# Four-block sequence model on one core: other work beside the first two and the last two scans

## The chip, the cores and the metric

The kernel runs on one core of one Trainium2 chip. The metric is device time in microseconds (us) of one execution. Its engines are TensorE (PE in the profile; PEld is its weight load), VectorE (DVE), ScalarE (ACT), GpSimd (POOL) and SyncE (SP), which here only issues DMAs.

## The reference, cut to what matters

Four blocks follow each other on x of 32 sequences, 256 positions, 256 channels, in float32. Each takes its scale, shift and gate from a condition vector. Blocks 1 and 3 are selective state-space layers (block 1 on permuted positions), 2 is softmax attention with 16 heads, 4 linear attention.

```python
def mamba(h):                                   # blocks 1 and 3
    xm, z = split(h @ W_in)                     # 512 channels each
    xm = silu(causal_conv4(xm) + conv_b)
    dtr, Bm, Cm = split(xm @ W_xp)              # 64, 16, 16
    dt = softplus(dtr @ W_dt + b_dt)
    def step(hst, t):                           # over 256 positions
        hst = hst * exp(dt[t] * A) + (dt[t] * xm[t]) * Bm[t]
        return hst, sum_over_16(hst * Cm[t])
    y = (scan(step) + xm * D) * silu(z)
    return y @ W_out
x = x + gate * unpermute(mamba(permute(mod(layernorm(x)))))    # block 1
x = x + silu(mod(layernorm(softmax(q @ k.T + mask) @ v))) @ W  # block 2
x = x + gate * mamba(mod(layernorm(x)))                        # block 3
x = x + silu(mod(layernorm(q_soft @ (k_soft.T @ v)))) @ W      # block 4
```

## The kernel before

The 32 sequences go in 16 groups of two (`NG = 16`), so a group's row of positions has 512 elements. Everything of a group stays in the core; each group passes through pieces of work:

- `front0` / `front1`: normalisation, input projection, convolution and silu of block 1 / block 3, in `front_tensor`, `front_scalar`, `front_vector` (lines 660 to 900).
- `mid0` / `mid1`: the projection w_xp (L722), its copy `xd` (L834), the rows B and C written to memory by SP (L1124), and the first of four step sizes `dt` (L886) and their products `dtx` (L909).
- `rest0` / `rest1`: the other three step sizes and the gate branch `sz` (L855).
- `scan0` / `scan1`: the recurrence of block 1 / block 3 in 32 steps. One step is, on DVE, a product with a slice of B (L1025) and a hardware scan (L1039), on ACT two exponentials (L975), on POOL the product with C (L1057) and an add (L1064), on PE an accumulation through the identity (L926). The slices of B and C come by DMA from memory, spread over the partitions (L1097). After each eight steps DVE gates a chunk of 128 channels (L1008).
- `back0` / `back1`: output projection (L1139), for block 1 the permutation back (L1149), gate (L1177) and residual sum (L1185).
- `attn_a` / `attn_b`: block 2 of the group's first / second sequence. A chain: statistics (L623), transposes (L1207), q, k, v (L1231, L1222), sixteen maxima of scores (L1277 on PE, L1397 on DVE), scores again transposed (L1304), exponentials (L1372), product with v (L1320), reciprocal (L1409), normalisation, output, and the sum into x_b (L1421).
- `lin_a` / `lin_b`: block 4 of the group's first / second sequence, with the result stored.

`scan0` and `scan1` alternate. A recurrence of one group is accompanied by other pieces of neighbouring groups. These stand in two lanes, `SIDE`; pieces of a lane follow each other and share its buffers. An entry is (piece, offset of its group from the iteration i, 0 or 1 for beside scan0(i) or scan1(i - 1)). In an iteration a piece whose group doesn't exist is left out, and so is a scan:

```python
SIDE = [[("attn_b", -1, 0), ("front1", -1, 0), ("back0", 0, 1), ("attn_a", 0, 1), ("front0", 1, 1)],
        [("rest0", 0, 0), ("back1", -2, 0), ("lin_a", -2, 0), ("mid1", -1, 0),
         ("rest1", -1, 1), ("lin_b", -2, 1), ("mid0", 1, 1)]]
SCAN = [("scan0", 0), ("scan1", -1)]
```

The order on each engine is fixed when the program is made. `PLACES[piece][engine]` has a number for each part of a piece, in units of scan steps: 8.4 stands between the operations of step 8. `iteration` merges the scan's own places (`AT`) with those of both lanes, smallest first. Every engine then works through its list strictly in order, waiting on semaphores for its inputs and for buffers. PLACES decides what may run beside what, and a part that waits holds up all behind it on its engine, the scan's steps included.

So before, back0(0), attn_a(0), front0(1) and mid0(1) stand in an iteration half in which scan1(-1) doesn't exist, and attn_b(15), front1(15), back1(14), lin_a(14) and mid1(15) in one in which scan0(16) doesn't exist. Where a scan has no successor beside it, its last two accumulations, its last POOL operations and its last gated product come at once.

`keep_result` (line 606) is a DMA that ACT issues, the copy of x_b, the attention's result, to `x_scratch` in memory; `back1` loads it again later. `scan_sync` issues the slices of B and C, `front_sync` the taps of the convolution and `mid_sync` the B and C rows, all on SP.

## Time and profile before

| | us |
|---|---|
| median of three runs | 5471.16 |
| the three runs | 5450.6, 5471.16, 5473.3 |
| the profiled execution | 5456.22 |
| its span, first to last instruction | 5454.5 |
| busy in it: PE, DVE, POOL, ACT | 4531.0, 4640.3, 4057.9, 3256.7 |

The span begins with a prologue and front0(0), mid0(0), up to the first step of scan0(0) at 122.3 us. Then 32 scans follow one another, the last of which ends at 5344.4. In the rows below the times count from the span's start, "granted clock" (PEclk) is the share of TensorE's full clock of 2.4 GHz that it had, a mean over the stretch where it changed in it (0.5 is the lower level of 1.2 GHz), and a figure in brackets with an arrow is the idle time of the engine ahead of an instruction and what ended it.

### The profile page before, as it was taken

The page shows a single profiled execution, that of the slowest core. Times are in us where ns is not written, and L with a number is a line of the kernel's source. Part 1 is how long each engine was busy: PE and PEld are TensorE (multiplying, and loading weights), DVE is VectorE, ACT ScalarE, POOL GpSimd, SP SyncE. Part 2 cuts the span into 40 slices and gives each one's busy share as a digit, 9 for nine tenths or more (in the row PEclk, how much of TensorE's full clock was granted, in tenths as well). Part 3 has the DMA queues.
Part 4 walks back from the last instruction along what each step waited for, and adds up shares of the span by engine and source line. Part 5 has one row for each costly group of instructions (what it writes and reads, how often), then busy time and mean ns, then how long its engine had stood idle before and what let it go on. Part 6 is the DMA issues. An engine that isn't in the chain of part 4 may idle for free.

```text
span 5454.5 us, 54997 instructions
## 1 busy us (share of the span) xinstructions
PE 4531.0 (83%) x16792; PEld 2409.9 (44%) x16792; DVE 4640.3 (85%) x4711; ACT 3256.7 (60%) x5572; POOL 4057.9 (74%) x2838
## 2 busy tenths in 40 slices
PE   4678888888888898888888888888889888888765
PEld 1243444444444444444444444444444444444423
DVE  2729899998999999999999999899999999999373
ACT  2336566666666666666666666666666666666252
POOL 1818787887878888787788788787878878787172
PEclk8668899999999999998999999999999999998776
DMA  4616666676766666676666667676666667666161
GB/s 144 221 44 233 224 237 223 232 240 215 240 214 240 229 232 229 226 252 220 229 224 236 230 232 239 217 244 214 239 229 234 229 225 250 218 229 219 45 206 58
DMA packets 355068, 1164.54 MB, mean 214 GB/s; under 512 B 39355, under 2 KB 79348, under 8 KB 354774
## 3 DMA queue, kind: packets, MB, share of 16 engines
q1 hardware_dynamic: 310614, 1106.42, 59.9%
q10 hardware_dynamic: 44160, 54.60, 3.1%
q8 instruction: 135, 2.21, 0.2%
q14 instruction: 159, 1.30, 0.1%
HBM read 1140.78 MB, written 20.10 MB: 213 GB/s over the span
## 4 chain that ended last, share of the span: by engine, by line
PE 43%; DVE 19%; POOL 11%; issue 10%; ACT 9%; DMA 5%; SPq 1%; DVEq 0%; POOLq 0%; ACTq 0%
DVE hw L1039 8%; PE ps L926 7%; PE ps L698 6%; POOL hw L1057 6%; PE ps L1231 5%; PE ps L1277 5%; PE ps L1304 4%; DVE ps L1025 3%; PE ps L1222 3%; POOL hw L1064 3%; DMA cs<-bc_scratch 2%; PE ps L1139 2%; PE ps L1320 2%; ACT da L975 2%; DVE mx L1397 2%
## 5 line engine op out<-in xcount | busy, mean ns | idle before, releaser
L1057 POOL TENSOR_TENSOR hw<-hw,cs 128x1024 f32<-128x1024 f32 x1024 | 2413.1, 2357 | 668.9 <-DVE hw L1039 604.2
L1039 DVE TENSOR_TENSOR_SCAN hw<-da,ps 128x1024 f32<-128x1024 f32 x1024 | 2333.4, 2279 | 66.1 <-ACT da L975 23.5
L975 ACT ACTIVATE da<-dt,a_neg 128x510 f32<-128x510 f32 x2048 | 1332.0, 711 | 175.2 <-DVE hw L1039 171.9
L1064 POOL TENSOR_TENSOR hw<-hw 128x512 f32<-128x512 f32 x1024 | 1298.1, 1268 | 66.3
L926 PE MATMUL ps<-hw,ident 128*128 128x512 f32 x2048 | 1177.7, 680 | 172.7 <-POOL hw L1064 172.7
L1025 DVE TENSOR_TENSOR ps<-ps,bs 128x1024 f32<-128x1024 f32 x1024 | 1255.9, 1226 | 38.8 <-ACT ps L989 11.3
L926 PEld LDWEIGHTS ps<-hw,ident 128*128 128x128 f32 x2048 | 398.6, 212 | 621.8 <-issue 322.6
L698 PE MATMUL ps<-hT,w_in 128*128 128x512 f32 x1024 | 532.7, 657 | 67.8 <-DVE dt L886 47.8
L1372 ACT ACTIVATE pts<-ps 128x512 f32<-128x512 f32 x512 | 278.5, 593 | 428.5 <-PE ps L1304 428.5
L1397 DVE TENSOR_REDUCE mx<-ps 128x2 f32<-128x512 f32 x512 | 330.9, 680 | 164.2 <-PE ps L1277 163.7
L1277 PE MATMUL ps<-k,q 32*128 32x256 f32 x2048 | 347.1, 464 | 106.1 <-DVE mx L1397 106.1
L570 ACT ACT_TABLE_LOAD x319 | 409.3, 1283 | 5.7
L698 PEld LDWEIGHTS ps<-hT,w_in 128*128 128x128 f32 x1024 | 200.4, 205 | 343.6 <-issue 208.8
L1277 PEld LDWEIGHTS ps<-k,q 32*128 32x128 f32 x2048 | 203.5, 214 | 298.8 <-DVE mx L1397 191.6
L1304 PE MATMUL ps<-q,k 32*128 32x256 f32 x2048 | 301.4, 413 | 15.4 <-ACT pts L1372 15.4
L1320 PE MATMUL ps<-pts,va 128*32 128x256 f32 x2048 | 271.2, 398 | 2.8 <-ACT pts L1372 2.8
L909 POOL TENSOR_TENSOR dtx<-dt,u 128x512 f32<-128x512 f32 x128 | 162.2, 1267 | 139.8 <-DVE dt L886 139.7
L1304 PEld LDWEIGHTS ps<-q,k 32*128 32x128 f32 x2048 | 180.9, 190 | 142.7 <-issue 60.2
L1139 PE MATMUL ps<-w_out,dtx 128*128 128x256 f32 x1024 | 240.2, 389 | 3.4 <-DVE dtx L1008 1.8
L713 PE MATMUL ps<-xd,w_dt 97*128 97x512 f32 x256 | 168.1, 744 | 76.8 <-POOL dtx L909 53.4
L707 PE MATMUL ps<-u,taps 128*128 128x512 f32 (+3 forms) x512 | 229.1, 590 | 0.0
L1139 PEld LDWEIGHTS ps<-w_out,dtx 128*128 128x128 f32 x1024 | 195.8, 194 | 57.6 <-issue 30.7
(178 smaller groups left out, 5296.6 us busy)
## 6 DMA issues: line engine op xcount, KB each, us to landing
bs<-bc_scratch SPq DMA_DIRECT2D x1024, 512.0 KB, 4.3
cs<-bc_scratch SPq DMA_DIRECT2D x1024, 512.0 KB, 4.9
taps<-taps_scratch SPq DMA_DIRECT2D x32, 512.0 KB, 5.6
xhat<-in_x ACTq DMA_DIRECT2D x16, 512.0 KB, 7.7
gate<-gates_scratch ACTq DMA_DIRECT2D x64, 128.0 KB, 5.1
x_b<-in_x ACTq DMA_DIRECT2D x16, 512.0 KB, 6.6
x_scratch<-x_b ACTq DMA_DIRECT2D x16, 512.0 KB, 2.9
x_c<-x_scratch ACTq DMA_DIRECT2D x16, 512.0 KB, 6.5
```

The lines of the kernel that those rows point to most:

```text
L570: nc.scalar.preload_act_table_set(name)
L698: ins = nc.tensor.matmul(side[pc.bank[f"m{m}"]], w_in[l][:, k, m * P:(m + 1) * P], hT[:, k, :], start=(k == 0), stop=(k == DC - 1))
L926: nc.tensor.matmul(yps, ident[:, :], hw[q % RING][:, 0, :], start=False, stop=(q % PER == PER - 1))\
L975: ins = nc.scalar.activation(da[q % (AHEAD + 1)][:, k, :, 1:S], dt_[:, c, :].rearrange("p (b s) -> p b s", b=GB)[:, :, 1:S], ACT.Exp, scal ...
L1025: nc.vector.tensor_tensor(z, dxp.unsqueeze(1).broadcast_to([P, 2, T]), bs[s % B_RING][:, :, :], ALU.mult)\
L1039: nc.vector.tensor_tensor_scan(tile[:, :, :].rearrange("p n t -> p (n t)"), da[s % (AHEAD + 1)][:, :, :, :].rearrange("p n b s -> p (n b s)"),
L1057: nc.gpsimd.tensor_tensor(tile[:, :, :], tile[:, :, :], cs[s % C_RING][:, :, :], ALU.mult)\
L1064: nc.gpsimd.tensor_tensor(tile[:, 0, :], tile[:, 0, :], tile[:, 1, :], ALU.add)\
L1139: ins = nc.tensor.matmul(side[pc.bank[key]][:, k * D:(k + 1) * D], dtx[l][:, c, r * P:(r + 1) * P], w_out[l][:, c, :], start=(c == 0), sto ...
L1277: ins = nc.tensor.matmul(banks[hh][:, t * S:(t + 1) * S], q4[rr, h // 4, t * P:(t + 1) * P], k4[rr, h // 4, :], start=True, stop=True)
L1304: ins = nc.tensor.matmul(banks[hh][:, t * S:(t + 1) * S], k4[rr, h // 4, t * P:(t + 1) * P], q4[rr, h // 4, :], start=True, stop=True)
L1397: nc.vector.tensor_reduce(mx[:, :, h // 4, at0], side[pc.bank[f"s{p}{hh}"]].rearrange("p (t s) -> p t s", t=RB), X, ALU.max, negate=True). ...
```

## The change

`SIDE`, `SCAN` and the iterations go. `PLAN` lists the segments one by one, each with its scan, its two lanes and the name of a table of places:

```diff
+def even(i):
+    return step((0, i), [("attn_b", i - 1), ("front1", i - 1)],
+                [("rest0", i), ("back1", i - 2), ("lin_a", i - 2), ("mid1", i - 1)], "even")
+def odd(i):
+    return step((1, i - 1), [("back0", i), ("attn_a", i), ("front0", i + 1)],
+                [("rest1", i - 1), ("lin_b", i - 2), ("mid0", i + 1)], "odd")
+PLAN = [odd(-1),
+        step((0, 0), [("front0", 1)], [("rest0", 0)], "first"),
+        step((0, 1), [("back0", 0), ("attn_a", 0), ("attn_b", 0), ("front1", 0)],
+             [("mid0", 1), ("rest0", 1), ("mid1", 0)], "second"),
+        odd(1)]
+for _i in range(2, NG - 1):
+    PLAN += [even(_i), odd(_i)]
+PLAN += [even(NG - 1),
+         step((1, NG - 2), [("back0", NG - 1), ("attn_a", NG - 1), ("attn_b", NG - 1), ("front1", NG - 1)],
+              [("rest1", NG - 2), ("lin_b", NG - 3)], "last_but_one"),
+         step((1, NG - 1), [], [("back1", NG - 2), ("mid1", NG - 1), ("rest1", NG - 1), ("lin_a", NG - 2),
+                                ("lin_b", NG - 2)], "last"),
+         step(None, [], [("back1", NG - 1), ("lin_a", NG - 1), ("lin_b", NG - 1)], "end")]
```

The tables "even" and "odd" have the numbers that `PLACES` had. "first", "second", "last_but_one", "last" and "end" are new, with places such as

```diff
+    "second": {
+        "mid0": {
+            "pe": [-100.8, -100.6, -100.4, -100.2, 0.208, 0.833],
+        "front1": {
+            "dve": [29.732, 29.866, 30.041, 30.082, 30.124, 30.165, 30.206, 30.247, 30.289],
```

where a negative place stands ahead of the scan's first step. Two more edits reach every scan:

```diff
@@ front_scalar
             ln_apply(act, lane_a, pc, g, lambda r: x_src[l][:, r, :], R)
-            if l == 1:
-                keep_result(act, g)
@@ mid_scalar, behind the copy xd
+            if l == 1:
+                keep_result(act, g)
@@ scan_vector and scan_sync
-            yield 0
+            yield -2
```

The second sorts the first B slice of a scan (place -0.8) ahead of pieces with a later negative place, on SP. The waits for shared buffers are written with one function, `prior(l, g)`, that names the recurrence before a given one, in place of `near`, `latest` and `before_scan`; they wait for what they waited for. `segment` merges places as `iteration` did, and `flush` has the last operations of a scan without a successor.

The order of instructions shows three places. On PE, from the end of scan0(0) to attention of group 0. Names: `hw` is the scan's tile, `w_xp` and `xd` belong to mid0(1), `w_out` and `xhat,onehot` to back0(0). Before:

```order
L941 MATMUL ps<-u,diag_d 128x512
L926 MATMUL ps<-hw,ident 128x512 x8
L1139 MATMUL ps<-w_out,dtx 128x256 x16
L1149 MATMUL ps<-xhat,onehot 128x256 x8
L1207 MATMUL ps<-ident,xhat 128x128 x4
```

After:

```order
L1121 MATMUL ps<-hw,ident 128x512 x7
L917 MATMUL ps<-u,w_xp 96x512 x4
L908 MATMUL ps<-xd,w_dt 128x512
L1334 MATMUL ps<-w_out,dtx 128x256 x16
L1344 MATMUL ps<-xhat,onehot 128x256 x8
L908 MATMUL ps<-xd,w_dt 128x512
```

mid0(1) has moved ahead of back0(0), and attention now begins behind the second low-rank product, beside scan0(1).

On DVE, attention into front of block 3, near the end of the packed scan0(1) (`mx` the maxima, `q` their sum into q, `rec` the reciprocal, `u` a convolution tap, `ps<-ps,bs` and `hw<-da,ps` a scan step). Before, of attn_a(0) and front0(1), in the stretch without a scan:

```order
L1397 TENSOR_REDUCE mx<-ps 128x2 x16
L1404 TENSOR_TENSOR q<-q,ps 128x512 x2
L1409 RECIPROCAL rec<-ps 128x16
L1411 TENSOR_TENSOR xhat<-ps,rec 128x256
```

After, of attn_b(0), front1(0) and mid1(0), in scan0(1):

```order
L1592 TENSOR_REDUCE mx<-ps 128x2 x13
L1599 TENSOR_TENSOR q<-q,ps 128x512 x2
L1220 TENSOR_TENSOR ps<-ps,bs 128x1024
L1234 SCALAR_TENSOR_TENSOR hw<-da,ps 128x1024
L1220 TENSOR_TENSOR ps<-ps,bs 128x1024
L1604 RECIPROCAL rec<-ps 128x16
...
L1073 SCALAR_TENSOR_TENSOR u<-ps,cols,u 128x2x253
L1234 SCALAR_TENSOR_TENSOR hw<-da,ps 128x1024
L1081 SCALAR_TENSOR_TENSOR dt<-ps,dt 128x512
L1220 TENSOR_TENSOR ps<-ps,bs 128x1024
L1234 SCALAR_TENSOR_TENSOR hw<-da,ps 128x1024
```

The links of the chain now alternate with scan steps; the scan's last three steps stand behind attn_b's reciprocals, front1's taps and mid1's dt.

On SP, where one scan passes into the next in the middle (`bc_scratch<-xd` writes the B and C rows, `bs` and `cs` are slices of them). Before:

```order
L1124 DMA bc_scratch<-xd 32x512
L1097 DMA cs<-bc_scratch 128x1024
L1114 DMA taps<-taps_scratch 128x1024
L1097 DMA bs<-bc_scratch 128x1024 x2
```

After:

```order
L1319 DMA bc_scratch<-xd 32x512
L1292 DMA cs<-bc_scratch 128x1024
L1292 DMA bs<-bc_scratch 128x1024
L1309 DMA taps<-taps_scratch 128x1024
L1292 DMA bs<-bc_scratch 128x1024
```

The load of the taps has moved behind the scan's first B slice.

## Rows read from the trace of the kernel before

**Rows 1.** Busy time by stretches: stretch, length, engines busy (instructions), clock, DMA share, GB/s.
```profile
core 0: us, PE busy (x) PEld busy (x) DVE busy (x) ACT busy (x) POOL busy (x), PEclk, DMA share, GB/s
122.30:244.40 122.10, 73.30 (x90) 21.13 (x88) 115.75 (x70) 56.60 (x84) 112.54 (x64) 0.61 0.81 271
244.40:395.60 151.20, 109.56 (x379) 62.38 (x380) 27.17 (x60) 35.33 (x67) 11.99 (x20) 0.67 0.05 16
395.60:542.50 146.90, 117.84 (x410) 55.91 (x408) 134.41 (x116) 91.45 (x154) 120.73 (x77) 0.86 0.70 239
2261.40:2412.90 151.50, 133.55 (x513) 70.26 (x513) 142.85 (x146) 98.34 (x173) 125.55 (x88) 0.94 0.68 239
2412.90:2573.10 160.20, 139.58 (x533) 76.90 (x533) 145.30 (x146) 105.05 (x178) 127.78 (x90) 0.92 0.66 223
4908.30:5062.10 153.80, 123.84 (x475) 68.35 (x475) 139.21 (x130) 91.24 (x156) 124.68 (x85) 0.84 0.66 223
5062.10:5208.10 146.00, 107.71 (x423) 61.37 (x423) 34.37 (x77) 46.44 (x89) 12.01 (x24) 0.78 0.08 25
5208.10:5344.40 136.30, 83.24 (x155) 34.41 (x155) 120.93 (x91) 68.14 (x106) 116.19 (x72) 0.68 0.73 244
```

**Rows 2.** The page's costliest groups: busy us, mean ns of one, idle before.
```profile
L1057 POOL TENSOR_TENSOR hw<-hw,cs 128x1024 f32<-128x1024 f32 x1024 | 2413.1, 2357 | 668.9 <-DVE hw L1039 604.2
...
L1064 POOL TENSOR_TENSOR hw<-hw 128x512 f32<-128x512 f32 x1024 | 1298.1, 1268 | 66.3
```

**Rows 3.** Timeline of DVE, first stretch without a scan: start, length, instruction.
```profile
264.69 0.70 DVE L1177 TENSOR_TENSOR ps<-ps,gate 128x512 f32<-128x512 f32 x1 [11.62 <-PE ps L1149]
...
267.87 0.75 DVE L623 BATCH_NORM_STATS2 stats<-x_b 128x6 f32<-128x256 f32 x2
...
352.17 0.69 DVE L1421 TENSOR_TENSOR x_b<-ps,x_b 128x512 f32<-128x512 f32 x1 [8.27 <-PE ps L1222]
357.09 1.41 DVE L623 BATCH_NORM_STATS2 stats<-xhat 128x6 f32<-128x256 f32 x4 [4.23 <-DMA xhat<-in_x]
...
381.42 2.31 DVE L878 SCALAR_TENSOR_TENSOR u<-ps,cols,u 128x510 f32<-128x510 f32 x3 [4.54 <-ACT u L779]
392.59 0.69 DVE L886 SCALAR_TENSOR_TENSOR dt<-ps,dt 128x512 f32<-128x512 f32 x1 [8.86 <-ACT dt L823]
...
395.56 1.23 DVE L1025 TENSOR_TENSOR ps<-ps,bs 128x1024 f32<-128x1024 f32 x1 [1.28 <-ACT ps L989]
```

**Rows 4.** Timeline of PE, same stretch: back0(0), then mid0(1).
```profile
253.22 9.61 PE L1139 MATMUL ps<-w_out,dtx 128*128 128x256 f32 x32 [0.88 <-DVE dtx L1008]
...
383.82 3.60 PE L722 MATMUL ps<-u,w_xp 128*96 128x512 f32 x8
388.10 1.12 PE L713 MATMUL ps<-xd,w_dt 97*128 97x512 f32 x2 [0.68 <-ACT xd L834]
```

**Rows 5.** Timeline of DVE, second stretch without a scan.
```profile
5069.14 0.74 DVE L623 BATCH_NORM_STATS2 stats<-x_b 128x6 f32<-128x256 f32 x2
...
5153.14 0.69 DVE L1421 TENSOR_TENSOR x_b<-ps,x_b 128x512 f32<-128x512 f32 x1 [5.61 <-PE ps L1222]
...
5201.05 0.69 DVE L886 SCALAR_TENSOR_TENSOR dt<-ps,dt 128x512 f32<-128x512 f32 x1 [9.03 <-ACT dt L823]
...
5208.12 1.22 DVE L1025 TENSOR_TENSOR ps<-ps,bs 128x1024 f32<-128x1024 f32 x1
```

**Rows 6.** Timeline of DVE: ends of two attention chains beside scans.
```profile
570.14 0.75 DVE L623 BATCH_NORM_STATS2 stats<-x_b 128x6 f32<-128x256 f32 x2
...
650.08 0.69 DVE L1421 TENSOR_TENSOR x_b<-ps,x_b 128x512 f32<-128x512 f32 x1 [2.32 <-PE ps L1222]
...
698.25 0.73 DVE L623 BATCH_NORM_STATS2 stats<-x_b 128x6 f32<-128x256 f32 x2
...
793.28 0.69 DVE L1421 TENSOR_TENSOR x_b<-ps,x_b 128x512 f32<-128x512 f32 x1
```

**Rows 7.** Waits of DVE from 1641.7 to 4442.8: total us, times, longest.
```profile
DVE ps L1025 <- DMA bs<-bc_scratch: 3.3, 9, 1.0
```

More of the change, by code:

```diff
@@ new lines, in step @@
+def step(scan, lane_a, lane_b, table):
+    lanes = [[(name, g) for name, g in lane if 0 <= g < NG] for lane in (lane_a, lane_b)]
+    return scan if scan and 0 <= scan[1] < NG else None, lanes, table
+def even(i):
[4 more added lines that the diff above has]
+                [("rest1", i - 1), ("lin_b", i - 2), ("mid0", i + 1)], "odd")
@@ L516, in build @@
         x_src, x_res = [xhat, x_b], [x_b, x_c]
-        near, table = {}, {}
+        table = {"now": None}
         def number(name, g):
```

533 lines of the change are left out of this document (344 added, 189 removed), and 18 rows, old and new, of the table PLACES.

## The prediction, made before the changed kernel ran

> **What bounds the kernel now.** I read the busy time by stretches first [rows 1]. The scans are the long stretches: in the middle one takes 151.5 to 160.2 us, with DVE busy for 142.9 and 145.3 of it, PE for 134 to 140 and POOL for 126 to 128. No engine is idle there for long, and only a small part of the change touches them. A scan alone has a floor: POOL's two operations for each of the 32 steps take 2.357 + 1.268 = 3.63 us, 116 us in all [rows 2], and scan0 of group 0, with only rest0 beside it, lasts 122.1 us [rows 1].
>
> The other thing in these rows is two stretches without any scan: 244.4 to 395.6 (151.2 us) and 5062.1 to 5208.1 (146.0 us). POOL works for 12.0 us in each, DVE for 27 and 34, DMA stands at 0.05 and 0.08. What runs is one chain, its links waiting for each other. I followed it on DVE, where each link leaves a row. In the first stretch: gate of back0 at 264.69, statistics of attn_a at 267.87, its result x_b finished at 352.17 + 0.69 = 352.9, so **85.0 us of attention chain**; front0 from 357.09 to the last convolution tap at 381.42 + 2.31 = 383.7, **26.6 us**; the step size dt at 392.59; the first step of scan0(1) at 395.56 [rows 3]. In the second: statistics of attn_b at 5069.14, result at 5153.8, 84.7 us; dt at 5201.05, first step of scan1(15) at 5208.12 [rows 5]. The change attacks exactly these, so its value is the length of the two stretches less what the packed scans grow.
>
> **How long a chain takes beside a scan** is the number on which everything rests, and before has it: attn_a of group 1 beside scan1(0) from 570.14 to 650.08 + 0.69 is 80.6 us, attn_b of the same group beside scan0(2) from 698.25 to 794.0 is 95.7 us [rows 6]. Bare it is 85. So a chain loses little to a scan beside it, and the scan goes on meanwhile. But one scan of 116 to 122 us cannot cover two such chains, a front and a mid: 85 + 85 + 27 + 9 is 206 us bare. Each packed scan ends when its chain does, not when POOL does.
>
> **Front of the program, part by part**, from the last step of scan0(0) at 244.4 to the end of the stretch at 542.5, where scan1(0) begins: 298.1 us before [rows 1]. After:
> (a) front0(1) moves beside scan0(0). On DVE it adds statistics 1.41, two small operations of about 0.5, and six taps at 2.31 / 3, 4.6 in all: 6.5 us [rows 3]. DVE was busy for 115.75 of 122.1 us and has no room for it, so +6.5 (2 if the waits hide it, 12 if taps wait for PE). Its work on PE and ACT (73.3 and 56.6 us busy there) is hidden; if that cover were gone, it would be the 26.6 us of the bare front.
> (b) The junction. Before, the last scan ends at 244.4 and the gate starts at 264.69, 20.3 us. Now PE has mid0(1) in front of back0: four projections and a low-rank product, 383.82 to 389.22, 5.4 us [rows 4], of which a little falls into the wait for the last gated product. I take +5. From gate to statistics it was 3.2 us; scan0(1)'s first multiplication (1.2 us) now stands between. Statistics start 30 us after the scan's end.
> (c) attn_a and attn_b one after the other. attn_a is paced by eight scan steps ahead of its first maxima, so I take 90, between 80.6 and 95.7. attn_b has its last twenty-odd DVE operations crowded between four scan steps and runs nearly bare: 88, between 84.7 and 95.7. Together 178 (161 to 191).
> (d) front1(0) has to end before the scan's step 30, since its taps stand ahead of it on DVE: 26.6 us bare, 30 with steps between (26 to 36, which is two and a half steps of 3.63 more).
> (e) mid1(0): last tap to dt 392.59 - 383.73 = 8.9, and dt to the next scan's first step 5208.12 - 5201.05 = 7.1 [rows 3, 5], under which the last scan step of 3.6 us is hidden.
> Sum 6.5 + 30 + 178 + 30 + 16 = 260.5. **Saved 37.6 us.** Nothing is gained twice: the 146.9 us of scan0(1) [rows 1] vanish into this chain.
>
> **End of the program**, from 4908.3 to 5208.1, 299.8 us before [rows 1]. After: three scan steps (11 us) and back0's gate and sums stand ahead of attn_a's statistics, with a wait for PE about 20 us (16 to 28). Then 178 for the two chains. Step 31 is done right after the second chain's result, so front1(15) runs bare but for that step: 30. New in the chain is back1(14), which DVE and PE have ahead of mid1(15): the last gated product 0.7, two groups of 16 products (9.61 us for 32, so 4.8 each) [rows 4], gate and sum 1.5 between them, since the second group waits for the first sum: 12. Then mid1: projections to dt 8.8, dt to the first step 3.0 [rows 3, 4]. Sum 20 + 178 + 30 + 12 + 11.8 = 251.8, **saved 48.0**. Against it, the last scan gets lin_a(14) beside lin_b(14). One lin chain and a different rest are what divides the last scan's 136.3 us from the first one's 122.1, so 14.2, while DVE's busy time differs by 5.2 only [rows 1]. The second lin costs between these: I take 11, nearer the whole. Net 37.0. The last stretch, 5344.4 to the end, holds the same chain in the same order: 0.
>
> **Middle.** On PE, DVE and POOL its instructions keep their order. On SP the first B slice of a scan is issued ahead of the taps; DVE waited for such a slice 9 times for 3.3 us in nine pairs of scans [rows 7], so at most some 5 us over the whole. On ACT the copy of x_b to memory comes after mid1's xd instead of after the front's normalisation. It lands there beside the write and the read of the B and C rows; it isn't waited for until the next back1. Its cover is the 0.66 to 0.68 share of DMA [rows 1]. I take -3 together (-5 to +15).
>
> **The sum.** 37.6 + 37.0 + 3 = 77.6 us. Against the profiled execution's own time, 5456.2 (span 5454.5), that is 5378.6. The three runs gave 5450.6, 5471.2 and 5473.3; the profiled one lies 15 us under their median. What is saved should carry over, so the forecast is 5471.2 - 77.6 = **5394 us** (1.4% less).
>
> **TensorE's clock** could move it. The granted clock is 0.67 and 0.78 in the two stretches without a scan, between the levels of 1.2 and 2.4 GHz, 0.86 in scan0(1) and 0.92 to 0.94 in the full middle scans [rows 1]: the busier PE is, the higher. That would speed the very links that move beside a scan. The Trainium skill, page "TensorE: Matmul & The Clock Gate", section "What's actually happening", says that the low clock is the default and that activity lifts it; these rows agree. By that rule alone all four chains would run as the quickest does, which is the first rival below.
>
> **Rivals.**
> 1. *Chains at the higher clock.* In a packed scan PE has work from the scan, rest, back, attention and front, and grants like the middle's 0.92. Then each chain takes the 80.6 us of [rows 6] rather than 90 and 88: 16.8 less in each of two packed scans, 33.6 together, 5360. For it speaks that table; against it, that 13 maxima in a row and the whole second half of attn_b's products stand on PE and DVE with hardly a scan step between, as bare as in the old stretch.
> 2. *Chains as slow as the slowest.* 95.7 us each, as attn_b beside scan0(2), where DVE's and ACT's order makes each link wait for scan steps: 13.4 more in each packed scan, and fronts of 36 rather than 30, 12 more: 5433. For it speaks that steps and links alternate in a fixed order; against it, that attn_b here has fewer steps among its links than in rows 6.
> 3. *Slower than before: the overlap fails.* Place: both packed scans. All engines work in a fixed order, and where a crowd of links stands ahead of a scan step, POOL runs dry and the steps come after the chain. My sum hides all 116 us of scan in each chain. What isn't hidden adds to the time: with half of it exposed, 2 x 58 = 116, 5510. It decides from one third exposed (78 of 232). Against it: rows 6, where scan and chain do go together, and bare chains of 85 that leave POOL idle.
> 4. *It touches the middle after all.* The copy to x_scratch meets the B rows at the start of 14 scans; at 1.5 us each that is 21 us, 5415. Rows 7 show how little slack a B slice has in every second scan; DMA at two thirds speaks against much.
>
> **How the numbers follow.** Chances: forecast 0.48, rival 1 0.20, rival 2 0.22, rival 3 0.04, rival 4 0.06. The terms of the forecast cannot all err the same way; two thirds of their spread give 5370 to 5420. The range reaches over rival 1's time and to rival 2's with its edges, 5340 to 5440. About 0.5% (27 us) is what a measurement of this kernel can tell from no change: under 5444 lie the forecast, rival 1, and most of 2 and 4: faster 0.88; the far edge of 2 and 4 gives same 0.08; slower 0.04 is rival 3.
>
> **What the changed kernel's profile would show.** Right: scan0(0) at 125 to 134 us; first to last step of scan0(1) some 215 to 235 us with the next scan starting near 505 instead of 542.5; scan1(14) some 190 to 205 us, scan1(15) at 141 to 150 us and beginning about 250 us after scan0(15) ends; attention chains of 80 to 96 us, back to back; middle scans as in rows 1 to a microsecond. Wrong: chains over 100 us (rival 2 or 3), POOL idle in long pieces with steps 25 to 31 stacked behind the chain and still to come after it, a granted clock over 0.9 with chains of 80 (rival 1), or middle scans longer by 1 us or more (rival 4).

## The result, and the profile after

The changed kernel takes 5421.34 us (median of six runs, 5411.25 to 5426.06); the kernel before, timed beside it, takes 5460.54 us (5448.15 to 5473.3). The ratio is 0.9925 with a 95% interval of 0.9908 to 0.9943: 39 us faster, where the forecast said 77.6. The time lies inside the predicted range. The profiled execution has a span of 5424.3 us against 5454.5, 30.2 us less and not 39, since the profiled run of before lies 4.3 us under its median and that of the changed kernel 4.7 above; a second trace of the changed kernel has a span of 5413.5 us. In what follows ratios are over the fast runs alone; one slow run each of e1 (6018.8 us) and e5 (6429.0 us) counts in their medians only.

Busy time of the changed kernel by stretches (columns as in [rows 1]): scan0(0); the junction; scan0(1) with both attention chains of group 0 and front1(0); the middle; scan1(14) with both chains of group 15; the stretch behind it; scan1(15). The last line is the middle of the kernel before.

```profile
core 0: us, PE busy (x) PEld busy (x) DVE busy (x) ACT busy (x) POOL busy (x), PEclk, DMA share, GB/s
126.30:248.70 122.40, 81.65 (x136) 30.51 (x136) 118.98 (x77) 65.85 (x96) 116.20 (x69) 0.74 0.79 266
248.70:270.60 21.90, 18.70 (x56) 11.08 (x57) 2.11 (x4) 5.58 (x9) 4.96 (x4) 0.83 0.33 109
270.60:513.30 242.70, 195.05 (x685) 97.82 (x683) 154.89 (x155) 114.64 (x194) 121.26 (x85) 0.77 0.41 141
515.40:4892.10 4376.70, 3809.93 (x14577) 2048.83 (x14577) 4026.54 (x4039) 2826.66 (x4847) 3541.50 (x2455) 0.93 0.68 230
4896.40:5129.90 233.50, 191.74 (x739) 108.91 (x739) 156.79 (x170) 100.84 (x185) 123.75 (x94) 0.77 0.42 141
5129.90:5175.00 45.10, 32.71 (x89) 17.37 (x90) 8.63 (x13) 13.23 (x23) 5.71 (x4) 0.88 0.18 63
5175.00:5318.70 143.70, 92.06 (x218) 45.95 (x217) 128.40 (x111) 76.94 (x129) 119.88 (x81) 0.74 0.68 229
...
542.50:4908.30 4365.80, 3805.72 (x14577) 2045.65 (x14577) 4026.60 (x4039) 2827.22 (x4846) 3540.83 (x2455) 0.93 0.68 230
```

The overlap is there: DVE and POOL now do a scan's work, 121 and 124 us of POOL, under the chains, and the long stretches in which POOL stood idle are gone. But the packed scans last 242.7 and 233.5 us, and the granted clock in both is 0.77, where a full middle scan has 0.92 to 0.94 [rows 1].

The chain's marks on DVE (start, length, instruction), as in [rows 3] and [rows 5]: statistics and result of attn_a(0) and attn_b(0), then of attn_a(15) and attn_b(15).

```profile
273.90 0.75 DVE L818 BATCH_NORM_STATS2 stats<-x_b 128x6 f32<-128x256 f32 x2
...
385.17 0.69 DVE L1616 TENSOR_TENSOR x_b<-ps,x_b 128x512 f32<-128x512 f32 x1 [1.48 <-PE ps L1417]
386.91 0.74 DVE L818 BATCH_NORM_STATS2 stats<-x_b 128x6 f32<-128x256 f32 x2
...
476.72 0.69 DVE L1616 TENSOR_TENSOR x_b<-ps,x_b 128x512 f32<-128x512 f32 x1 [5.89 <-PE ps L1417]
...
4920.94 0.75 DVE L818 BATCH_NORM_STATS2 stats<-x_b 128x6 f32<-128x256 f32 x2
...
5030.93 0.67 DVE L1616 TENSOR_TENSOR x_b<-ps,x_b 128x512 f32<-128x512 f32 x1
5032.64 0.74 DVE L818 BATCH_NORM_STATS2 stats<-x_b 128x6 f32<-128x256 f32 x2
...
5124.97 0.69 DVE L1616 TENSOR_TENSOR x_b<-ps,x_b 128x512 f32<-128x512 f32 x1 [8.27 <-PE ps L1417]
```

attn_a(0) takes 112.0 us and attn_b(0) 90.5; attn_a(15) takes 110.7 and attn_b(15) 93.0. The forecast had 90 and 88. So the first block's chain is 22.0 and 20.7 us too long in the two packed scans, 42.7 us of the 47.4 by which the traces fall short of the forecast. The table behind the experiments has the other terms.

One term came out near the forecast's size, but for another reason. The chain that leads to the first step of scan0(0) (start, length, what):

```profile
116.92 7.44 DMA xhat<-in_x
...
124.48 1.42 DVE stats L818 x4
...
126.36 1.12 DVE ps L1220
```

front0(1) now has its statistics on DVE ahead of the first scan step, and they wait for its input, which lands at 124.4. scan0(0) begins at 126.3 instead of 122.3.

### The profile page after: what moved, and what is told of

Its sections match the earlier page's. It is cut to its first block, busy times and chain, and to the rows that moved or that the text cites. A ratio compares the mean times of both kernels' runs of the same rounds, so it can differ in the third digit from the quotient of the medians.

```text
span 5424.3 us, 55001 instructions
## 1 busy us (share of the span) xinstructions
PE 4533.2 (84%) x16792; PEld 2421.1 (45%) x16792; DVE 4642.0 (86%) x4711; ACT 3257.2 (60%) x5574; POOL 4057.2 (75%) x2838
## 4 chain that ended last, share of the span: by engine, by line
PE 44%; DVE 20%; POOL 11%; issue 10%; ACT 9%; DMA 5%; SPq 1%; DVEq 0%; ACTq 0%; POOLq 0%
DVE hw L1234 8%; PE ps L1121 8%; PE ps L893 6%; POOL hw L1252 5%; PE ps L1426 5%; PE ps L1472 5%; PE ps L1499 4%; DVE ps L1220 3%; PE ps L1417 3%; POOL hw L1259 3%; PE ps L1515 2%; PE ps L1334 2%; ACT da L1170 2%; DVE mx L1592 2%; DMA cs<-bc_scratch 2%
## 5 line engine op out<-in xcount | busy, mean ns | idle before, releaser
L902 PE MATMUL ps<-u,taps 128*128 128x512 f32 (+3 forms) x512 | 231.1, 594 | 0.0
L1334 PEld LDWEIGHTS ps<-w_out,dtx 128*128 128x128 f32 x1024 | 192.8, 191 | 60.2 <-issue 32.3
```

Of the source, the lines that this page charges most:

```text
L1334: ins = nc.tensor.matmul(side[pc.bank[key]][:, k * D:(k + 1) * D], dtx[l][:, c, r * P:(r + 1) * P], w_out[l][:, c, :], start=(c == 0), sto ...
```

## The experiments

Two theories stood at the start. The first: a chain's links take their turn in a fixed order behind the scan's steps and other pieces, on DVE, ACT and PE alike, and the first block's chain has more of that beside it. The second: PE sets the chain's pace, by its clock and by the scan's sums. Beside them stood the question of the middle, 10.9 us longer. Differences of packed scans under 4 us are not read: a second trace of the same kernel (the last but one run below) moves that much.

**e1, e2: each end alone.** The lines of `PLAN` are those of after at one end and those of before at the other.

```diff
 PLAN += [even(NG - 1),
-         step((1, NG - 2), [("back0", NG - 1), ("attn_a", NG - 1), ("attn_b", NG - 1), ("front1", NG - 1)],
...
+         odd(NG - 1),
+         step(None, [("attn_b", NG - 1), ("front1", NG - 1)], [("back1", NG - 2), ("lin_a", NG - 2), ("mid1", NG - 1)],
```

> Only the front is rearranged; the last two groups' scans and chains keep the order of the kernel before. Theory by stretches (the traces of before and after, added up): the prologue gives back 4.0 us and the stretch between the first two scans saves 31.4, so 27 us in all, 5433 against 5460. Rival A, the moved copies and pieces inside the unchanged middle cost the 10.9 us by which that middle grew: this kernel has them too, so it saves 16 us, about 5444. Rival B, the forecast on record: 37.6 us, 5423. The middle of the trace tells A from the first theory: 4366 or 4377 us from the start of the second layer's first scan to the end of the last scan of the first layer. The attention chain of block 0 beside the scan should again take 108 to 116 us and that of block 1 88 to 93, since nothing in the front differs from after.

> Only the end is rearranged; the front keeps the order of the kernel before. Theory by stretches: the stretch between the last scan of the first layer and the last scan saves 16.9 us, the last scan costs 7.4, what follows it saves 4.5: 14 us, 5446 against 5460. Rival A, the grown middle (10.9 us) belongs to the moved copies: 3 us, 5457. Rival B, the forecast on record: 37 us, 5423. The chain of block 0 of the last group should again take about 110 us and that of block 1 about 93.

Front alone: ratio 0.996 (0.9945 to 0.9976), 5440.7 us against 5459.6; scan1(0) begins at 514.1 us, 28.4 earlier than before. End alone: 0.9989 (0.9968 to 1.001), 5456.6 us; from the end of scan0(15) to the end of the last scan 426.1 us for 436.1, and 105.6 for 110.1 behind it. These marks repeat those of after to 2 us, and by them the front has two thirds of the saving. The medians add up to 22 us of after's 39; the three intervals are too wide to call that a difference, and the end alone can't be told from no change by its time. The chains come out as in after: 109.2 and 90.3 us in e1, 110.7 and 93.0 in e2. (After's own second trace, e11 below, has 109.2 where its first had 112.0.)

**e3: the middle's moved pieces moved back.** The copy of x_b returns to front1, and the scan's two generators begin at 0 again.

```diff
             ln_apply(act, lane_a, pc, g, lambda r: x_src[l][:, r, :], R)
+            if l == 1 and 0 < g < NG - 1:
+                keep_result(act, g)
...
-            yield -2
+            yield 0
```

> After with the middle's copies as in the kernel before: the result rows are kept from the second layer's front, not from its middle piece, and the scan's pieces on VectorE start where they did. Theory A (the moved copies and pieces cost what the middle grew by): the stretch from the first scan of the second layer to the last scan of the first layer, 4376.7 us in after and 4365.8 in before, is 4363 to 4368 and the kernel 10 us faster than after, 5408 to 5414. Theory B (the 10.9 us are scatter between executions: the runs with the moved copies so far show 4369.7, 4372.0 and 4363.4, those without 4365.8 and 4368.5): anywhere from 4362 to 4378, and no difference in time that can be told from after.

(The text on record counts e2 among the kernels without the moved copies; e2 has them.) The middle takes 4376.8 us, as in after, and the kernel 5417.5 us, ratio 0.9918 (0.9896 to 0.994). Theory A's 4363 to 4368 did not come: taking the moved copy and the moved starts back does not by itself shorten the middle. That they cost nothing is not shown by it, as e10 and e12 below show.

**e5: the two chains spread evenly over scan0(1).**

```diff
+EVENLY = {"second": [(2.0, 2.0), (20.0, 14.5), (28.75, 26.0), (31.0, 30.4)], ...
+for _p in ("attn_a", "attn_b", "front1"):
+    for _e in PLACES["second"][_p]:
+        PLACES["second"][_p][_e] = [evenly(x, EVENLY["second"]) for x in PLACES["second"][_p][_e]]
```

> After with the places of both attention chains and of the second layer's front in the scan of the second group stretched anew, so that they spread evenly over its 32 steps (block 0 over some 12 steps where after has 18, block 1 over 12 where it has 9, the front over 4 where it has 1). Theory 1 (order: block 0's links wait behind the steps put between them): block 0's chain falls from 112 to 92 to 97 us, block 1's rises from 91 to 93 to 97, the packed scan from 242.7 to 222 to 232 us, the kernel to 5402 to 5412. Theory 2 (TensorE's time: it is busy 195 of the 242.7 us, and the work it does for the scan costs the same wherever it stands): what block 0 gains block 1 loses, the packed scan stays within 238 to 246 us, the kernel 5417 to 5425.

Both theories missed: 5445.9 us, ratio 0.998 (0.9963 to 0.9998), and the packed scan takes 262.2 us. attn_a(0) takes 109.3 us, no less than in after's second trace (109.2), although 16 scan steps stand among its links instead of 21; attn_b(0) loses 12.3 (102.8) with 12 for 9, and from its result to scan1(0) it is 46.4 us for 38.0. For the first stage of attn_a(0), from statistics to the first maximum, the windows of after and of e5 and the wait of DVE in e5 are:

```profile
273.90:306.60 32.70, 26.99 (x84) 14.44 (x84) 32.08 (x23) 29.55 (x47) 28.95 (x20) 0.95 0.72 245
...
273.20:308.80 35.60, 28.60 (x80) 15.45 (x81) 25.06 (x20) 26.14 (x42) 27.63 (x19) 0.81 0.59 201
...
DVE mx L1611 <- PE ps L1491: 10.1, 1, 10.1
```

In after DVE is busy for 32.1 of 32.7 us with nine scan steps ahead of the first maximum. With seven steps ahead it is done earlier and then waits 10.1 us for the scores. So the order on DVE hid a second limit of about the same length: PE's, which waited there for ScalarE's sz of rest0(1) (5.1 us) and for dt (2.8 us) before it came to the chain's products.

**e6, e9: ScalarE's table loads.** In that stage ACT loads a function table eight times, 1.283 us each, for the four SiLU of rest0(1) between exponentials. Here the SiLU of this one piece are plain copies (e6), and the same together with the even order (e9).

```diff
-                tables(SILU)
+                plain = l == 0 and isinstance(g, int) and g == 1
+                if not plain:
+                    tables(SILU)
```

> After with the second group's gate branch (the four activations of sz in the piece rest0 beside the scan of group 1) as plain copies instead of SiLU, so that part of the computation is changed; it takes away the eight loads of ScalarE's function table (10.3 us) that fall into the first 33 us of block 0's chain, 273.9 to 306.6 us. Theory S (this stage is ScalarE's and VectorE's, 29.6 and 32.1 us busy of 32.7, and the table loads take ScalarE from both the scan's decays and the chain's copies): the stage falls from 32.7 to 22 to 26 us, block 0's chain from 112.0 to 101 to 106, the packed scan from 242.7 to 232 to 237, the kernel by 6 to 10 us against after. Theory V (the chain waits there for the scan steps that are put ahead of it on VectorE, and ScalarE would only idle): the stage stays over 30 us and the kernel where after is.

> The kernel in which both chains spread evenly over the second group's scan (packed scan 262.2 us, block 0's first stage 35.6 us although its links stand earlier), and with it the second group's gate branch as plain copies instead of SiLU, which changes part of the computation and leaves out six function table loads (7.7 us) of that stage. Theory Q (a chain's link takes its turn behind what stands ahead of it on each engine's queue: in after that is the scan's sums on TensorE, in the even order TensorE's own wait of 5.1 us for sz behind ScalarE's table loads): the first stage falls from 35.6 to 26 to 30 us, block 0's chain from 109.3 to 99 to 104, the packed scan from 262.2 to 252 to 257; without the even order the same copies had changed nothing (32.6 for 32.7). Theory N (the first stage is bounded by the scan's own pace on VectorE and GpSimd in either order): it stays at 33 us or more, and the packed scan over 259. By both the kernel stays slower than after, since block 1's chain and the front behind it keep their steps of the scan.

The stage in e6, and what DVE waited for in e9's:

```profile
273.10:305.80 32.70, 29.27 (x85) 15.41 (x85) 32.05 (x24) 21.51 (x41) 30.40 (x21) 0.90 0.76 257
...
DVE mx L1614 <- PE ps L1494: 5.0, 1, 5.0
```

e6: ACT is busy 8 us less, the stage is 32.7 us as in after, attn_a(0) takes 109.1 us (109.2 in after's second trace), the kernel 5424.0 us with a ratio of 0.9928 (0.9902 to 0.9954): theory V. e9: with the even order the same loads do count, 30.5 us for 35.6 in the stage, and the wait for scores is halved; the packed scan of 259.3 us is still longer than after's (the kernel takes 5444.6 us, ratio 0.9957, 0.9941 to 0.9974), and the sizes fall short of what theory Q expected (26 to 30 and 252 to 257). So neither limit alone is worth anything, and both taken away bring the stage 2.2 us under after's.

**e7: PE's share of the scan cut.**

```diff
-            nc.tensor.matmul(yps, ident[:, :], hw[q % RING][:, 0, :], start=False, stop=(q % PER == PER - 1))\
+            packed = isinstance(g, int) and (l, g) in ((0, 1), (1, NG - 2))
+            w = S if packed else T
+            nc.tensor.matmul(yps[:, 0:w], ident[:, :], hw[q % RING][:, 0, 0:w], start=False,
```

> After with the scan's sums over states on TensorE cut from 512 to 256 columns in the two packed scans (group 1 of the first layer, the last group but one of the second), so part of the sum is left out. By the rows of both shapes (about 680 and 380 ns) that is 0.3 us for each of 32 sums, 10 us of TensorE in each packed scan. Theory T (the chain beside the scan is TensorE's: busy 32.7 of the 37.2 us of the exponential stage with a mean of 838 ns for a sum): block 0's exponential stage falls from 37.2 to 31 to 34 us, its whole chain from 112 to 103 to 108, each packed scan by 6 to 10 us, the kernel by 12 to 20. Theory O (what costs is that steps of the scan stand between the chain's links on ScalarE and VectorE, whatever TensorE does): the chains change by under 3 us and the kernel by under 5.

The exponential stage of attn_a(0) falls to 31.3 us, within theory T's bounds (after: 37.2, in its second trace 34.8), and the chain to 107.1. The packed scan falls to 236.8, 3 to 6 us shorter, and scan1(14) to 231.1, no less than in after's second trace; the kernel takes 5421.0 us, ratio 0.9918 (0.9893 to 0.9943). So PE's work for the scan is part of that stage's length and little of the whole. What the stage gained the first stage lost, 37.7 us for 32.7: the 16 k products took 7.6 us there (654 ns each), the 16 q products before them 3.6 (379 ns). They have the same shape; the granted clock of the whole stage fell to 0.82, from 0.95 in after.

**e4, e8: the clock.** Ahead of the pairs of 32-row products stands one full matmul (four instructions in the trace), whose result is overwritten: in e4 ahead of all score pairs and transposed pairs of the four chains, in e8 ahead of block 1's four transposed pairs only.

```diff
+                    if b == 1 and g in (0, NG - 1):
+                        nc.tensor.matmul(banks[0][:, 0:S], ident[:, :], onehot[:, 0, :], start=True, stop=True)
```

> After with one more matmul of 128 rows, 128 columns of weights and 256 columns ahead of each of the four pairs of score products and of the four pairs of transposed ones, in all four chains (two blocks of the first and of the last group); its result is overwritten. The eight matmuls of a chain cost 3 to 6 us of TensorE by the rows of that shape (379 to 484 ns at the mean clock, up to twice as much at the lower level). Theory 1 (order: block 0's links are queued behind steps of the scan): chains 3 to 6 us longer, the granted clock of the stretches unchanged, the kernel 5421 to 5445. Theory 2 (clock: products of 32 rows and sums into 32 columns leave the granted clock at 0.50 to 0.60, and block 0's chain beside a scan takes 112 us because each of its matmuls and each of the scan's takes longer there): the granted clock of the pv stages rises from 0.50 to 0.8 or more, block 0's chain falls from 112 to 95 to 102 us, block 1's from 91 to 75 to 82, the kernel to 5365 to 5390.

> After with the additional matmul (128 rows, 128 columns of weights, 256 columns; overwritten) only ahead of the four pairs of transposed score products of block 1, in the first and in the last group, where the run with it everywhere had the granted clock at 0.88 for 0.53 and the stage at 27.3 and 25.8 us for 32.3 and 32.4. Theory C (the clock sets this stage, and nothing else is late with it): both stages again 25 to 28 us, all other stages as in after within 1 us, the packed scans 236 to 239 and 227 to 229 us, the kernel 9 to 12 us faster than after. Rival D (the engine spends elsewhere what it gains, as in the run with the matmul everywhere, whose packed scan took 246.6 us): the packed scans within 2 us of 242.7 and 233.5, the kernel where after is.

The exponential stage of attn_b(0) in after, then in e8 and e4:

```profile
432.00:466.20 34.20, 33.66 (x140) 15.91 (x141) 5.93 (x6) 10.21 (x20) 0.00 (x0) 0.53 0.13 46
...
429.00:458.20 29.20, 27.66 (x152) 13.65 (x152) 4.72 (x5) 10.02 (x20) 0.00 (x0) 0.83 0.17 54
...
441.60:468.90 27.30, 25.51 (x151) 12.93 (x151) 4.63 (x3) 10.03 (x20) 0.00 (x0) 0.90 0.19 59
```

(Counted as in the table of stages, from the end of the additions into q, after's is 32.3 us.) More work on PE, and less time: with the clock at 0.83 to 0.90 instead of 0.53 the stage is 3 to 5 us shorter, and the same stage of attn_b(15) takes 25.8 us in e4 and 27.5 in e8, 32.4 in after. That much of theory 2 holds, though e8's 29.2 is outside the 25 to 28 expected. But e4 as a whole takes 5434.2 us, ratio 0.9955 (0.9936 to 0.9974), and its packed scans 246.6 and 229.5 us: in attn_a(0) the stage has a clock of 0.76, no more than after's two traces (0.72 and 0.80), and its four additional matmuls take 5.7 us of PE (42.6 us for 37.2), where the text on record priced all eight of a chain at 3 to 6. The expected 95 to 102 us for that chain (116.5 measured) falls, and so do the 75 to 82 for block 1's (90.6 and 90.2). e8, with the matmul only where nothing stands beside the chain, has packed scans of 235.9 and 228.6 us, as theory C expected, 4 to 7 and 3 to 5 less than in the two traces of after, at the edge of what is read; its time, 5424.6 us with a ratio of 0.9939 (0.9916 to 0.9962), can't be told from after's.

**e10, e11, e12: three edits together, and after once more.** e10 is e8 with e3's middle, and one link moved: beside scan1(14) block 0's second addition into q goes one scan step forward on DVE.

```diff
+PLACES["last_but_one"]["attn_a"]["dve"][19] = 9.9
```

> After with three edits at once, each with its own place in the trace: the additional matmul ahead of block 1's four transposed score pairs in the first and last group (as in the clock run with it there alone), the middle's copies as in the kernel before, and, beside the last scan but one, the second addition into q of block 0 on VectorE placed ahead of the next scan step instead of behind one more (place 9.9 for 10.665). Theory Q (order on the queue): the stage between the last maximum and the end of both additions, 10.1 us in after and 1.9 in a bare chain, falls by one step of the scan, 3.5 us, to 6 to 7 us, and block 0's chain from 110.7 to 106 to 108; rival: the addition waits there for TensorE's transposes, which stand behind the scan's sums, and VectorE's next step with it: the stage stays at 9.5 to 10.5. The additional matmul again brings block 1's exponential stage to 27 to 30 us. The middle brings nothing that can be told from scatter. Packed scans 234 to 238 and 224 to 228 us, the kernel 5404 to 5414, against 5421 of after.

> After itself once more, beside the others on one chip: how far its trace and its time move from one execution to the next. By the scatter of the seven variants: the middle stretch 4363 to 4384 us (4376.7 the first time), block 0's chain in the second group 108 to 113 us, block 1's 90 to 91, the packed scan 239 to 243, the time 5415 to 5427. If the middle again takes 4376 to 4378 and block 0's chain 112, the small differences between variants are worth reading; if not, nothing under 4 us of a packed scan or 10 us of the middle is.

DVE around that link, in after and in e10:

```profile
4979.90 0.69 DVE L1599 TENSOR_TENSOR q<-q,ps 128x512 f32<-128x512 f32 x1 [2.58 <-PE ps L1482]
4980.50 2.28 DVE L1234 TENSOR_TENSOR_SCAN hw<-da,ps 128x1024 f32<-128x1024 f32 x1
4982.82 1.23 DVE L1220 TENSOR_TENSOR ps<-ps,bs 128x1024 f32<-128x1024 f32 x1
4983.98 0.69 DVE L1203 TENSOR_TENSOR dtx<-ps,sz 128x512 f32<-128x512 f32 x1
4984.59 2.28 DVE L1234 TENSOR_TENSOR_SCAN hw<-da,ps 128x1024 f32<-128x1024 f32 x1
4986.78 0.66 DVE L1599 TENSOR_TENSOR q<-q,ps 128x512 f32<-128x512 f32 x1
...
4945.44 0.69 DVE L1606 TENSOR_TENSOR q<-q,ps 128x512 f32<-128x512 f32 x1 [2.23 <-PE ps L1487]
4946.05 2.28 DVE L1239 TENSOR_TENSOR_SCAN hw<-da,ps 128x1024 f32<-128x1024 f32 x1
4948.24 0.66 DVE L1606 TENSOR_TENSOR q<-q,ps 128x512 f32<-128x512 f32 x1
```

A link that had two scan steps ahead of it now has one. The stage between the last maximum and the second addition goes from 10.1 us to 5.7, a little under the 6 to 7 of theory Q; the next stage takes 35.2 us instead of 31.3, so that the chain, at 108.5 us, is just over the 106 to 108 expected and no shorter than the 107.6 of after's second trace. In e12, the same kernel once more, the two stages take 5.6 and 36.9 us and the chain 110.0. What the link gained was given back.

The kernel e10 takes 5402.5 us, ratio 0.9879 (0.9853 to 0.9905); after in the same comparison 5429.7 us, 0.9929 (0.9905 to 0.9952), span 5413.5. The kernel's gain is more than the edits' own stages show: the packed scans are 236.8 and 227.5 us, against 239.6 and 231.6 in e11, and the middle is 4352.5 us, against 4373.0. So it was run again.

> The kernel with the three edits once more. In its first trace the packed scans were 236.8 and 227.5 us (239.6 and 231.6 in the second trace of after) and the middle 4352.5 us, the shortest of all, where after had 4373.0. Theory S (the edits are worth what their own stages show, about 3 and 4 us, with 1 us of the last scan; the middle's 20 us are scatter): the packed scans again 236 to 238 and 227 to 229, the middle 4363 to 4385, the kernel 5408 to 5424. Theory M (copies as before and edits together really shorten the middle): the middle again under 4360 and the kernel 5398 to 5407. A third: the middle is over 4363 in the trace and the time still under 5407, in which case the one trace says little of the runs.

It took 5401.9 us, ratio 0.9896 (0.9878 to 0.9913), with packed scans of 236.1 and 231.9 us and a middle of 4352.7: theory M, but for the second packed scan, which is no shorter than after's 231.6. The three edits make the fastest kernel here, 19 to 28 us under after by the medians (of the ratios' intervals, e10's ends where after's begin, e12's overlaps them slightly), and most of that lies in the middle, where one edit alone (e3, 4376.8) and another alone (e8, 4383.5) gave none.

The middle over all fourteen traces runs from 4352.5 to 4384.7 us. Among those with after's order in it it runs from 4363.3 (e5) to 4384.7 (e9), among the three with e3's order from 4352.5 (e10) to 4376.8 (e3). Two traces of one kernel agree: 4376.7 and 4373.0 for after, 4352.5 and 4352.7 for e10 and e12. The waits for the B and C slices differ too. From 545 to 4830 us, the groups (busy, mean ns, idle before) of after and of e12:

```profile
L1252 POOL TENSOR_TENSOR hw<-hw,cs 128x1024 f32<-128x1024 f32 x876 | 2064.8, 2357 | 601.9 <-DVE hw L1234 537.6 <-DMA cs<-bc_scratch 46.5 <-DVE ps L1220 15.4
...
L1220 DVE TENSOR_TENSOR ps<-ps,bs 128x1024 f32<-128x1024 f32 x876 | 1074.0, 1226 | 37.0 <-DMA bs<-bc_scratch 15.9 <-ACT ps L1184 8.4 <-ACT da L1170 0.3
...
L1257 POOL TENSOR_TENSOR hw<-hw,cs 128x1024 f32<-128x1024 f32 x881 | 2078.6, 2359 | 583.7 <-DVE hw L1239 529.2 <-DMA cs<-bc_scratch 37.8 <-DVE ps L1225 14.5
...
L1225 DVE TENSOR_TENSOR ps<-ps,bs 128x1024 f32<-128x1024 f32 x881 | 1080.0, 1226 | 32.7 <-DMA bs<-bc_scratch 11.9 <-ACT ps L1189 7.1 <-ACT da L1175 0.8
```

Added up for both engines, the waits for slices are 47.6 us in before, 49.7, 52.5 and 60.8 in the three traces with e3's order (e12, e10, e3), and 62.4 to 80.9 in the ten traces with after's. So the moved copy and starts do go with longer waits. The length of the middle follows the waits only loosely: the two longest middles have the two largest sums (e8 79.9, e9 80.9), but e5 has 72 us of waits in 4363.3 us and e3 60.8 in 4376.8. In the middle e8 and e10 differ by nothing but this order, and there it goes with 31 us (4383.5 and 4352.5), where between after and e3 it goes with none. Why a kernel lands at one end or the other is not settled; no run separates it.

## Why the prediction was right and wrong, step by step

Measured against the forecast's own terms, from the two first traces:

| term | forecast | measured |
|---|---|---|
| front0(1) beside scan0(0) | +6.5 | +4.3 (4.0 of it ahead of the scan) |
| end of scan0(0) to statistics of attn_a(0) | 30 | 25.2 |
| both chains of group 0 | 178 | 203.5 |
| from there to scan1(0) | 46 | 38.0 |
| **front, saved** | **37.6** | **27.1** |
| end of scan0(15) to statistics of attn_a(15) | 20 | 28.8 |
| both chains of group 15 | 178 | 204.7 |
| from there to scan1(15) | 53.8 | 49.3 |
| last scan | +11 | +7.4 |
| **end, saved** | **37.0** | **9.5** |
| middle | -3 | +10.9 |
| last stretch | 0 | -4.5 |
| **sum** | **77.6** | **30.2** |

**The mechanism was right, the size was half.** The two stretches without a scan disappear under the chains, each packed scan ends with its chain, and the gain is the difference; e1 and e2 show each end's part in the trace when it is made alone. The packed scans, 242.7 and 233.5 us, are longer than the 215 to 235 and 190 to 205 written down, and scan1(15) begins 283 us after scan0(15) ends, for 250. The third rival (overlap fails) is out. The single pieces, front0(1), the junction at the front, front1 with mid1, back1 and the second lin, came out within 9 us each, mostly below the forecast. Two were off in kind. The 4 us of front0(1) are not the taps' time on DVE but a wait for its input at the scan's very start. And at the end the statistics come 8.8 us later than said: 4.3 of these 28.8 us pass before the scan's first step at 4896.4.

**The step that failed is (c), the length of a chain beside a scan**, and its twin at the end: 25.5 and 26.7 us too short, 52 us together, more than the whole miss of 47.4. Nearly all of it is block 0: 112.0 and 110.7 us for the 90 of the forecast, where block 1's 90.5 and 93.0 stayed inside its 84.7 to 95.7.

The forecast took 90 for block 0 as a value between the two chains of [rows 6]. These two differ in the number of scan steps that stand among their links: 15 in the chain of 80.6 us, 20 in that of 95.7. attn_a(0) has 21 in after, so its nearest row was the slow one, and a choice between rows cost 5.7 of the 22 us. The other 16 lie outside all rows. Against attn_b(1) of before, the chain of 95.7 us, they are 11.3 in the first stage (32.7 for 21.4), where nine steps stand ahead of the first maximum instead of five, at nearly the same clock; 8.3 in the stage of the exponentials (37.2 for 28.9), with a granted clock of 0.72 for 1.00; 2.8 in the output, and 6 less in the two stages between. The two stages in attn_b(1) of before:

```profile
698.30:719.70 21.40, 19.48 (x68) 11.59 (x68) 19.57 (x18) 16.85 (x34) 21.06 (x17) 0.92 0.77 277
...
753.70:782.60 28.90, 28.00 (x170) 16.05 (x171) 27.77 (x25) 20.04 (x40) 25.97 (x19) 1.00 0.79 268
```

The number of steps alone does not set the length either: e5 has 16 among attn_a(0)'s links and takes 109.3 us. The first rival (chains at the higher clock) named one of the two quantities and assumed the wrong value for it: 0.77, not 0.92. The second rival's total, 38 us saved, is the one that was measured, but its working isn't: it had 95.7 for each chain and longer fronts, where the trace has 112 and 90 with fronts shorter than the forecast's. The written sign of being wrong, "chains over 100 us", is what the trace shows for block 0.

Where the 27 us over a bare chain lie in attn_a(0), by stage (statistics to first maximum; maxima; the additions into q; exponentials with both products; output). First the bare chain of the kernel before, then after; the first stage of after is shown above, with e5:

```profile
267.90:288.10 20.20, 15.24 (x55) 10.89 (x55) 1.03 (x5) 6.60 (x16) 1.26 (x4) 0.75 0.00 0
288.10:307.50 19.40, 13.69 (x61) 7.97 (x60) 10.29 (x17) 0.00 (x0) 0.00 (x0) 0.61 0.00 1
307.50:309.40 1.90, 1.82 (x8) 1.41 (x10) 1.28 (x3) 0.00 (x0) 0.00 (x0) 0.50 0.00 0
309.40:341.40 32.00, 30.34 (x134) 14.04 (x131) 0.02 (x1) 10.22 (x20) 0.00 (x0) 0.52 0.00 1
341.40:352.90 11.50, 6.04 (x17) 3.71 (x15) 3.02 (x10) 3.39 (x5) 1.24 (x4) 0.59 0.00 0
...
306.60:332.60 26.00, 21.53 (x76) 10.25 (x74) 20.02 (x26) 8.68 (x13) 15.01 (x10) 0.71 0.46 149
332.60:334.50 1.90, 1.89 (x8) 1.47 (x10) 1.28 (x3) 0.00 (x0) 0.58 (x1) 0.50 0.65 248
334.50:371.70 37.20, 32.74 (x148) 14.46 (x146) 25.08 (x15) 19.23 (x35) 23.94 (x13) 0.72 0.54 187
371.70:385.90 14.20, 9.40 (x25) 4.86 (x24) 12.27 (x17) 7.23 (x10) 11.41 (x10) 0.76 0.48 173
```

The first stage costs 12.5 us of the 27, at a granted clock of 0.95 for the bare chain's 0.75. It is a matter of order, as e5, e6 and e9 show: DVE's nine steps stand ahead of the first maximum, and right behind this limit stands PE's queue with rest0(1) on it. "attn_a is paced by eight scan steps" stood in the forecast; its price, 9 steps of DVE in 32.7 us where the bare stage needs 20.2, was never put into the sum. The maxima cost 6.6, the exponential stage 5.2, the output 2.7. (After's second trace has 34.8 us for 37.2 in the exponential stage and the same elsewhere, so some 2.5 of the 27 us move from execution to execution.)

In the exponential stage the clock has its part. PE's groups in it (busy, mean ns, idle before), and those of the same stage of attn_b(1) in the middle, which has a granted clock of 1.00, as many products and a scan beside it, and takes 28.6 us:

```profile
L1499 PE MATMUL ps<-q,k 32*128 32x256 f32 x62 | 12.2, 526 | 4.5 <-ACT pts L1567 4.5
L1515 PE MATMUL ps<-pts,va 128*32 128x256 f32 x64 | 11.1, 505 | 0.0
L1121 PE MATMUL ps<-hw,ident 128*128 128x512 f32 x14 | 10.1, 838 | 0.0
...
L1515 PE MATMUL ps<-pts,va 128*32 128x256 f32 x64 | 7.8, 385 | 0.0
...
L1499 PE MATMUL ps<-q,k 32*128 32x256 f32 x52 | 7.4, 398 | 0.2 <-ACT pts L1567 0.2
L1121 PE MATMUL ps<-hw,ident 128*128 128x512 f32 x12 | 6.5, 627 | 0.0
```

A product takes 526 ns for 398, 505 for 385, a sum 838 for 627. Brought to the same counts (7.4 x 62/52 = 8.8, 6.5 x 14/12 = 7.6) PE is busy 33.4 us for 24.2 with this work: 9 us, about the 8.6 by which the stages differ. That the clock is what makes the products longer is read from this comparison; e4, which tried to raise it here, got 0.76 and did not test it. e7 shows PE's share from the other side: with half of each sum the stage takes 31.3 us. It isn't the clock alone: e5 has 0.80 here with four steps, and 37.1 us, where after's second trace has 0.80 and 34.8.

At the end, attn_a(15) loses elsewhere: 10.4 us in the maxima (29.8), where lin_b(13)'s links stand between them on PE and DVE, 8 us at the additions into q (10.1), which are the two scan steps in the rows of e10 above, and 6 in the first stage. The stage of the maxima has 29.8 us at a granted clock of 0.53, 25.9 at 0.69 in after's second trace and 24.5 at 0.96 in e4, so about half of its excess goes with the clock; how much of the rest is lin_b wasn't tried alone.

**The middle** was forecast at -3 (-5 to +15). It came at +10.9 in the first trace, inside the range. The 3 us gained were to be DVE's waits for B slices; these grew instead, here from 545 to 4830 us in before and in after:

```profile
DVE ps L1025 <- DMA bs<-bc_scratch: 7.1, 14, 1.6
...
DVE ps L1220 <- DMA bs<-bc_scratch: 15.9, 21, 2.4
```

They are 15.3 us and more in all ten traces with after's order and 8.7 to 13.2 in the three of e3, e10 and e12. So the fourth rival's mechanism is seen in the waits, while what it costs in time stays open: taken back alone (e3) it gave nothing, taken back in e10 the middle is 31 us shorter than e8's. With one order of instructions in it the middle varies by 21 and 24 us from kernel to kernel, more than this term ever was, and that scatter should have stood in the range.

**The clock's rule.** The prediction cited the Trainium skill, page "TensorE: Matmul & The Clock Gate", section "What's actually happening", that the low clock is the default and activity releases it, and said that the rows agree. The rows of the packed scans don't agree with how the first rival read it: PE is busy for 33.66 of 34.2 us in attn_b(0)'s exponential stage at a granted clock of 0.53, and busy for 27.66 of 29.2 at 0.83 in e8. The measurement decides.

That the range held is partly luck: the forecast's own spread was 5370 to 5420, and it was the second rival, whose working did not come true, that had pulled the upper edge to 5440. By the two traces the saving is 30 us, by the medians 39. The median of before, 10.6 us lower in this comparison than in the three runs of the forecast, helped a little: taken from 5460.5, the forecast would have been 5383.

## What to carry to other kernels

Price a chain that moves beside other work stage by stage, at the clock and in the queue that it will have there. Count the other work's steps ahead of its first link and between its links, and start from a covered chain with the same count; here a bare run and two covered runs, one with fewer steps, did not enclose the new one. On each engine ask what is late next when one limit goes; here taking limits away gained 2 us of a stage or nothing three times over (e6, e9, e10). And before a term of a few microseconds in a long unchanged stretch is explained, trace the same kernel twice and a neighbour once: here a middle with the same instructions moved by over 20 us.

## What the runs showed of the hardware

- TensorE at 95 to 98% busy with products of 32 rows and sums into 32 columns kept a granted clock of 0.53 to 0.57 (33.66 of 34.2 us at 0.53; 30.43 of 32.1 at 0.57 in e11). Four full 128-row matmuls in between, 16 instructions of 380 ns (the median), brought it to 0.83 to 1.00 and made the stage 3 to 7 us shorter in e4, e8 and e10, and to 0.78 with less than 1 us gained in one stage of e12.
- The clock is not the same in each execution: the exponential stage of attn_b(15) had 0.92 and 27.7 us in e10, 0.78 and 31.6 us in e12, with one and the same kernel, and attn_a(15)'s stage of the maxima 0.53 and 29.8 us, then 0.69 and 25.9, in after's two traces.
- One form of matmul in one stage differed by nearly two: 16 products of hT_a with a mean of 379 ns, then 16 more with 654 ns, in e7; the granted clock was 0.91 up to the first of the slower ones (274.8 to 300.0 us) and 0.64 from there (to 312.5).
- A function table load takes 1.283 us of ScalarE; leaving out those of rest0(1) in a stage of 33 us gained nothing where VectorE was the limit (e6), and 5 us where it wasn't (e5 and e9, 35.6 and 30.5 us).
